# Rows transposed unscaled, mask tiles among the projections, and w1's product from high and low parts

## The reference

```
weights = x @ router_w + router_b            # per token
topi    = top 512 tokens of each batch; 511 of them, sorted, are selected
x_sel   = x[sel];  w_sel = weights[sel];  m_sel = mask[sel, sel]
hn      = x_sel * rsqrt(mean(x_sel^2) + 1e-6) * ln1
q, k, v = rope(hn @ wq), rope(hn @ wk), hn @ wv       # 16 heads of 16
o       = softmax(q k^T / 4 + m_sel) v @ wo
x1      = x_sel + o
x2      = x1 + gelu(rmsnorm(x1, ln2) @ w1) @ w2       # w1: 256 x 1024
out     = LayerNorm(x + scatter(x2 * w_sel) + x * (1 - sel_mask))
```

## Time and profile before

| | |
|---|---|
| median of 3 runs | 522.49 us (522.30 to 522.64) |
| profiled execution: its time, its span | 524.21 us, 522.5 us |
| PE busy | 437.1 us (84%) |
| PEld busy | 322.6 us (62%) |
| DVE busy | 389.2 us (74%) |
| ACT busy | 288.0 us (55%) |
| POOL busy | 173.0 us (33%) |
| chain that ended last, by engine | PE 39%, issue 14%, DVE 12%, POOL 9%, ACT 5% |
| chain, by line (largest) | L905 9%, L974 6%, L920 5%, L892 5%, L981 4% |

### The profile page before, as it was taken

How to read it: one execution, slowest core, us unless ns; L and a number is a source line. 1 busy time by engine, 2 the same in 40 slices (tenths; PEclk the granted TensorE clock), 3 DMA queues, 4 the chain that set the end, 5 groups by cost and what they waited for, 6 DMA issues and landing times.

```text
span 522.5 us, 9872 instructions
## 1 busy us (share of the span) xinstructions
PE 437.1 (84%) x3362; PEld 322.6 (62%) x3362; DVE 389.2 (74%) x1212; ACT 288.0 (55%) x611; POOL 173.0 (33%) x210
## 2 busy tenths in 40 slices
PE   3698999897999532698888999998998999997970
PEld 3487888786888422565675666664685666663560
DVE  2787888799888789667379999958368999956050
ACT  2335646444654460015688999944577999942200
POOL 9156677676767630552223000001000000003231
PEclk9999999998999855599998999998999999997995
DMA  7713432342231210249640000000000000000100
GB/s 224 235 42 82 123 120 82 118 124 81 82 121 42 80 41 1 85 150 316 204 134 2 1 3 3 3 1 0 1 1 2 2 2 3 1 2 10 32 30 11
DMA packets 29913, 33.90 MB, mean 65 GB/s; under 512 B 6404, under 2 KB 25512, under 8 KB 29864
## 3 DMA queue, kind: packets, MB, share of 16 engines
q1 hardware_dynamic: 23088, 24.78, 14.6%
q0 software_dynamic: 3520, 8.40, 5.4%
q10 hardware_dynamic: 3256, 0.10, 0.4%
HBM read 19.63 MB, written 13.63 MB: 64 GB/s over the span
## 4 chain that ended last, share of the span: by engine, by line
PE 39%; issue 14%; DVE 12%; POOL 9%; ACT 5%; another core or an unknown queue 1%; POOLq 1%; DVEq 0%; ACTq 0%
PE ps L905 9%; PE ps L974 6%; PE ps L920 5%; PE ps L892 5%; PE ps L981 4%; POOL arena L493 3%; PE ps L842 3%; PE ps L861 3%; POOL r L502 1%; PE ps L756 1%; POOL h_parts L552 1%; POOL rq L507 1%; PE ps L846 1%; DVE arena L1337 1%
## 5 line engine op out<-in xcount | busy, mean ns | idle before, releaser
L1184 ACT ACTIVATE arena<-arena,nmax 128x511 f32<-128x511 f32 x128 | 91.6, 720 | 5.6 <-DVE nmax L1609 5.3
L1609 DVE CUSTOM_DVE_ANT_0 arena<-ps,nmask 128x511 f32<-128x511 f32 x128 | 84.8, 684 | 0.2 <-DVE nmask L1557 0.2
L905 PE MATMUL ps<-ident,arena 128*128 128x128 f32 x512 | 80.0, 279 | 2.8 <-ACT big L397 1.1
L905 PEld LDWEIGHTS ps<-ident,arena 128*128 128x128 f32 x512 | 60.0, 142 | 24.5 <-ACT arena L1184 13.4
L683 PE MATMUL ps<-wgd_hi,x_hi 128*128 128x512 f32 x128 | 51.9, 405 | 0.0
L892 PE MATMUL ps<-arena 96*128 96x512 bf16 x128 | 49.1, 389 | 1.9 <-DVE nmask L1557 1.1
L684 PE MATMUL ps<-wgd_lo,x_hi 128*128 128x512 f32 x128 | 50.6, 395 | 0.0
L685 PE MATMUL ps<-wgd_hi,x_lo 128*128 128x512 f32 x128 | 50.5, 395 | 0.0
L397 DVE COPY big<-ps 128x512 f32<-128x512 f32 x64 | 44.1, 689 | 5.2 <-PE ps L905 3.9
L493 POOL TENSOR_TENSOR arena<-arena 128x512 f32<-128x512 f32 x32 | 41.2, 1290 | 12.7 <-DVE arena L1288 11.1
L397 ACT COPY big<-ps 128x512 f32<-128x512 f32 x64 | 37.0, 577 | 8.3 <-PE ps L920 6.6
(11 more groups left out here) (236 smaller groups left out, 994.5 us busy)
## 6 DMA issues: line engine op xcount, KB each, us to landing
arena<-in_L_attn_x SPq DMA_DIRECT2D x16, 512.0 KB, 4.6
out<-ob_sb SPq DMA_DIRECT2D x16, 512.0 KB, 3.2
w_sb<-in_L_ffn_w SPq DMA_DIRECT2D x2, 1024.0 KB, 11.5
mt_scratch<-nmask SPq DMA_DIRECT2D x8, 256.0 KB, 3.0
mt_scratch<-big SPq DMA_DIRECT2D x8, 256.0 KB, 3.8
big<-in_L_attn_Wg SPq DMA_DIRECT2D x1, 256.0 KB, 4.3
big<-in_L_attn_WD SPq DMA_DIRECT2D x1, 256.0 KB, 4.9
wqk<-in_L_ffn_wq SPq DMA_DIRECT2D x1, 256.0 KB, 8.8
```

What stands on the lines that cost most here:

```text
L905: mm = pe.transpose(ps[:, 2 + u % 2, k * P:(k + 1) * P], pr[u % 4][:, k * P:(k + 1) * P], ident[:, :])
L1184: act.activation(pr[u % 4][:, 0:K - 1], sm[u % 4][:, 0:K - 1], ACT.Exp, bias=nmax[:, c, h:h + 1], scale=-1.0, accum_out=rsum[:, c, h:h + 1 ...
L1609: dve.tensor_tensor_reduce(sm[u % 4][:, 0:K - 1], ps[:, S_BANKS[u % AHEAD], 0:K - 1], nmask[b][:, c, 0:K - 1], 1.0, 3.4e38, ALU.add, ALU.m ...
```

## The change

It does four things. The gathered rows are transposed as they come (`x_sel` in place of `hn`), and the factor per row (`wf_sel[..., 2]`, one per partition) is multiplied in by the copies of q, k (ACT) and v (DVE) out of PSUM; `first_normalised` goes, and `copy_qk` gets a wait for `angle_ready[b]`. `one_hots` builds `at_lo` and the two values of the row numbers first, `at_hi` next and the other 13 values last, and POOL starts the gathers on the first index tile. The mask's tiles of batch 0 are put among batch 1's first projections, in three banks; chunks 2 and 3 of batch 1 are transposed ahead of batch 1's tiles. The product with w1 is made of three float32r terms from `w1_hi`, `w1_lo` and `hnT_hi`, `hnT_lo`; the first two blocks have their low term last. The scratch of the selection moves from `qk[0]` to `v_sb[1]` and `x_sel[1]`.

```diff
+        w1_lo, = under(("w1_lo", [P, KD, F], F32R))
         w1_sb = sb("w1_sb", [P, KD, F])
+        w1_hi = sb("w1_hi", [P, KD, F], F32R)
...
+        hnT_hi, = under(("hnT_hi", [P, KD, K], F32R))
         hnT = sb("hnT", [P, KD, K])
+        hnT_lo, = under(("hnT_lo", [P, KD, K], F32R))
         qk = [sb(f"qk{b}", [P, C, 2 * D]) for b in range(B)]
         hi_rep = qk[1][:, :, :].rearrange("p c d -> p (c d)").bitcast(BF16)[:, 0:P * NT].rearrange("p (h n) -> p h n", h=P)
-        early_qk = qk[0][:, :, :].rearrange("p c d -> p (c d)")
+        v_sb = [sb(f"v_sb{b}", [P, C, D]) for b in range(B)]
 
         def scratch(at, n, dt=F32):
-            return early_qk[:, at:at + n].bitcast(dt)
+            tile, at = (v_sb[1], at) if at < 992 else (x_sel[1], at - 992)
+            return tile[:, :, :].rearrange("p c d -> p (c d)")[:, at:at + n].bitcast(dt)
...
-        R_BANK, REST_BANK = (2, 0), (4, 1)
+        R_BANK, REST_BANK = (2, 0), (1, 1)
+        X_BANK = ((2, 3), (3, 3))
...
-            pool.wait_ge(rows_ready[0], 3)
...
             def kept(b):
-                pool.wait_ge(hn_ready[b], C)
+                pool.wait_ge(angle_ready[b], 1)
                 for c in range(C):
+                    pool.wait_ge(x_sel_in[b][c], 16)
                     pool.tensor_scalar(keep[b][:, c, :], x_sel[b][:, c, :], wf_sel[:, b, c, 1:2], keep_m[:, b, c:c + 1],
...
-            gather_x(0)
-            gather_mask_rows(0)
-            pool.wait_ge(rows_ready[1], 3)
-            gather_x(1)
-            gather_mask_rows(1)
-            gather_mask_columns(0)
-            gather_mask_columns(1)
+            for b in range(B):
+                pool.wait_ge(rows_ready[b], 1)
+                gather_x(b)
+                pool.wait_ge(rows_ready[b], 2)
+                gather_mask_rows(b)
+            for b in range(B):
+                pool.wait_ge(rows_ready[b], 3)
+                gather_mask_columns(b)
...
-                pe.wait_ge(lo_ready[b], 1)
+                pe.wait_ge(lo_ready[b], 1 if hi == 2 else 2)
...
+                if b > 0:
+                    pe.wait_ge(angle_ready[b - 1], 1)
...
-            def turn_mask_rows(b):
+            def turn_mask_rows(b, tiles):
                 pe.wait_ge(m_rows_in[b], 16 * C)
-                for n in range(MS // P):
+                for n in tiles:
                     tile = n + b * (MS // P)
-                    if n == 0:
-                        pe.wait_ge(hnT1_ready[b], C)
-                    if b == 0 and n == 2:
+                    if tile == 0:
+                        pe.wait_ge(hnT1_ready[0], C)
                         pe.wait_ge(angle_ready[1], 1)
-                    if tile >= 4:
-                        pe.wait_ge(mT_ready[(tile - 4) // (MS // P)], (tile - 4) % (MS // P) + 1)
+                    elif tile >= 3:
+                        pe.wait_ge(mT_ready[(tile - 3) // (MS // P)], (tile - 3) % (MS // P) + 1)
                     for c in range(C):
-                        mm = pe.transpose(ps[:, (n + 2) % 4, c * P:(c + 1) * P], m_rows[b][:, c, n * P:(n + 1) * P], ident[:, :])
+                        mm = pe.transpose(ps[:, tile % 3, c * P:(c + 1) * P], m_rows[b][:, c, n * P:(n + 1) * P], ident[:, :])
                     mm.then_inc(mT_done[b], 1)
...
             def turn_first_hn(b, c):
-                pe.wait_ge(hn_ready[b], c + 1)
-                if c + b * C >= 2:
-                    pe.wait_ge(hnT1_ready[(c + b * C - 2) // C], (c + b * C - 2) % C + 1)
-                if b > 0:
-                    pe.wait_ge(mT_ready[b - 1], MS // P)
+                pe.wait_ge(x_sel_in[b][c], 16)
+                if b == 0 and c >= 2:
+                    pe.wait_ge(hnT1_ready[0], c - 1)
+                elif b == 1:
+                    pe.wait_ge(hnT1_ready[1], c)
                 for k in range(KD):
-                    mm = pe.transpose(ps[:, 2 + c % 2, k * P:(k + 1) * P], hn[:, c, k * P:(k + 1) * P], ident[:, :])
+                    mm = pe.transpose(ps[:, X_BANK[b][c % 2], k * P:(k + 1) * P], x_sel[b][:, c, k * P:(k + 1) * P], ident[:, :])
                 mm.then_inc(hnT1_done[b], 1)
...
             def hidden(b):
-                for f in range(FB):
-
-                    if f >= 2:
-                        pe.wait_ge(gelu_ready, b * FB + f - 1)
+                def with_high(f):
                     for k in range(KD):
                         pe.wait_ge(hnT_ready, b * KD + k + 1)
-                        mm = pe.matmul(ps[:, 4 + f % 2, :], w1_sb[:, k, f * P:(f + 1) * P], hnT[:, k, :],
-                                       start=(k == 0), stop=(k == KD - 1))
+                        for w in (w1_hi, w1_lo):
+                            pe.matmul(ps[:, 4 + f % 2, :], w[:, k, f * P:(f + 1) * P], hnT_hi[:, k, :],
+                                      start=(k == 0 and w is w1_hi), stop=False)
+
+                def with_rest(f):
+                    for k in range(KD):
+                        pe.wait_ge(hnT_lo_ready, b * KD + k + 1)
+                        mm = pe.matmul(ps[:, 4 + f % 2, :], w1_hi[:, k, f * P:(f + 1) * P], hnT_lo[:, k, :],
+                                       start=False, stop=(k == KD - 1))
                     mm.then_inc(h1_done, 1)
+
+                pe.wait_ge(w1_lo_ready, KD)
+                for f in range(2):
+                    with_high(f)
+                for f in range(2):
+                    with_rest(f)
+                for f in range(2, FB):
+                    pe.wait_ge(gelu_ready, b * FB + f - 1)
+                    with_high(f)
+                    with_rest(f)
...
-            turn_mask_rows(0)
-            for c in range(2):
+            turn_mask_rows(0, range(3))
+            turn_first_hn(1, 0)
+            project(1, range(1))
+            turn_mask_rows(0, range(3, 5))
+            turn_first_hn(1, 1)
+            project(1, range(1, 2))
+            turn_mask_rows(0, range(5, 8))
+            for c in range(2, C):
                 turn_first_hn(1, c)
-            for c in range(2):
-                project(1, range(c, c + 1))
-                turn_first_hn(1, 2 + c)
-            turn_mask_rows(1)
+            turn_mask_rows(1, range(8))
+            pe.wait_ge(hnT1_ready[1], C)
             pe.wait_ge(mT_ready[1], MS // P)
...
+            for k in range(KD):
+                act.wait_ge(w_ready, k + 1)
+                act.copy(w1_hi[:, k, :], w1_sb[:, k, :]).then_inc(w_ready, 1)
...
             def copy_hnT(b):
                 for k in range(KD):
                     act.wait_ge(hnT_done, b * KD + k + 1)
-                    act.copy(hnT[:, k, :], ps[:, 2 + k, :]).then_inc(hnT_ready, 1)
+                    act.copy(hnT_hi[:, k, :], ps[:, 2 + k, :]).then_inc(hnT_ready, 1)
 
             def copy_qk(b, c):
                 act.wait_ge(qk_done[b], c + 1)
-                act.copy(qk[b][:, c, :], ps[:, 4 + c % 2, :]).then_inc(qk_ready[b], 1)
+                act.wait_ge(angle_ready[b], 1)
+                act.mul(qk[b][:, c, :], ps[:, 4 + c % 2, :], wf_sel[:, b, c, 2:3]).then_inc(qk_ready[b], 1)
...
-                    act.mul(m_turned[b][n], ps[:, (n + 2) % 4, :], -1.0).then_inc(mT_ready[b], 1)
+                    act.mul(m_turned[b][n], ps[:, (n + b * (MS // P)) % 3, :], -1.0).then_inc(mT_ready[b], 1)
...
-            sines(0)
             for c in range(2):
                 copy_first_hnT(0, c)
+            sines(0)
             copy_qk(0, 0)
             for c in range(2, C):
                 copy_first_hnT(0, c)
                 copy_qk(0, c - 1)
             copy_qk(0, C - 1)
+            copy_mask_rows(0, range(3))
+            copy_first_hnT(1, 0)
+            copy_qk(1, 0)
+            copy_mask_rows(0, range(3, 5))
+            copy_first_hnT(1, 1)
+            more_parts(0, 0)
+            copy_qk(1, 1)
+            copy_mask_rows(0, range(5, 8))
+            for c in range(2, C):
+                copy_first_hnT(1, c)
+            copy_mask_rows(1, range(5))
+            more_parts(0, 1)
+            copy_mask_rows(1, range(5, 8))
             sines(1)
-            copy_mask_rows(0)
-            for c in range(2):
-                copy_first_hnT(1, c)
-            more_parts(0, 0)
-            for c in range(2):
-                copy_first_hnT(1, 2 + c)
-                copy_qk(1, c)
-            more_parts(0, 1)
-            copy_mask_rows(1)
...
             def one_hots(b):
-                dve.tensor_tensor(at_hi[:, b], slot_b[:, b, 0:1, :].broadcast_to((P, P, NT)), hi_rep[:, :, :],
-                                  ALU.is_equal).then_inc(at_ready[b], 1)
                 step.link(dve.tensor_tensor(
                     at_lo[:, b], slot_b[:, b, 1:2, :].broadcast_to((P, C, NT)),
                     lo_row[:, :].rearrange("p (c o) -> p c o", o=1).broadcast_to((P, C, NT)), ALU.is_equal))
+
+                def place(v0, v1):
+                    dve.tensor_tensor(
```

(47 more changed lines are left out.)

8 lines of the change are left out of this document (4 added, 4 removed).

## The result

The change made the kernel faster, by less than was forecast. Nine runs of the new kernel have a median of 519.19 us (516.68 to 521.22), nine of the old one beside them 522.49: a ratio of 0.9939 [0.9918, 0.9961], 3.3 us less where 8.2 were predicted. 519.19 lies 0.6 above the range. The profiled execution took 517.93 us (span 516.2, mean granted clock 0.931).

What follows compares the result with a forecast made beforehand. PE alone was taken to bound the product with w1, a chain walking between engines the stretch from the picks; 3.8 (Parts 1 and 2) + 2.3 + 2.3 = 8.4, taken as 8.2, gave 514.3 us, range 511.0 to 518.6.

Steps and rivals of the forecast that it cites:

- Part 3: Product with w1: three float32r products take 0.70 us where a float32 one took 0.86; 2.3 us less per batch, 4.6 in all.
- in either kernel: Product with w1: both stretches begin at the low clock, which costs some 2 us in the old and the new kernel.
- one that was too small (0.35): Product with w1: new wait of 0.35 us per batch, as gelu of block 0 needs its low term first.
- The cover of `rest_of_w1`: DVE before 349.20: two subtractions, 2.4 us together, fit in 3.07 us of idle, with 0.6 of room.
- Rival (b): The front's gain comes, the product's does not, as gelu or the low clock eats it: 518.7 us, chance 0.05.
- (d): Product with w1: weight loads and float32r products don't overlap, so the change is slower: 529.6 us, chance 0.03.
- Part 1: Picks of batch 0 to its transposes: first projection 4.4 us earlier, PE at the mask's tiles 3.7 earlier (235.5).
- Part 2: Mask's tiles: new order 18.7 us, 1.3 more than before, from a start 5.1 earlier; `turn_split(0, 0)` at 255.0, 3.8 earlier.
- an ACT that idled 7.50 us until 240.68 with a releaser that the profile doesn't know: Mask's tiles: the old first copy waited for this ACT idle, so the start gains more than PE does.
- From `turn_split(0, 0)` to attention nothing changes but the start.: Behind the mask's tiles: the 3.8 us gained up to `turn_split(0, 0)` carry on to attention unchanged.
- a clock that stays low past 224: Sign in the profile after, early projections: a clock still low past 224 us would show the forecast wrong.
- Rival (a): Front's gain swallowed by a wait in the interleaved mask part, later clock rise or ACT idle: 517.9 us, chance 0.14.

Runs made afterwards that it cites:

- product_only: The kernel before with only the product with w1 made of float32r terms, its front the old one: 518.16 us, ratio 0.9909.
- spread_gap_turns: The changed kernel with batch 1's picks spread among batch 0's projections and 16 unneeded transposes before the first `turn_split`: 514.60 us, ratio 0.985 to the kernel before.
- r_before: The kernel before, run again without edit: 522.70 us, ratio 1.0007.
- front_only: The changed kernel with the old float32 product with w1: 523.58 us, ratio 1.0013 to the kernel before.
- r_after: The changed kernel, run again without edit: 519.45 us, ratio 0.9935 to the kernel before.
- old_order: The changed kernel with the mask's tiles and batch 1's projections in the old order on PE and ACT: 516.71 us, ratio 0.9874 to the kernel before.
- front_old_order: The changed kernel with only the early transposes and `one_hots`: old float32 product, mask's tiles in the old order: 520.86 us, ratio 0.9963 to the kernel before.
- spread_old_order: The changed kernel with batch 1's picks spread and the mask's tiles in the old order: 514.22 us, ratio 0.9857 to the kernel before.

## Why the prediction was right and wrong

**Part 3 was right in its sum, partly by luck.** 4.6 us were forecast and `product_only` has 4.8, give or take 1. Products lie 0.23 us apart as in the earlier trace rows, and 48 take 13.2 us as forecast, where the stretch begins at the low clock. But the low clock doesn't cost 2 us "in either kernel". In the first batch of `spread_gap_turns` the clock is 1.00 throughout and the 48 products still take 367.50 - 355.00 = 12.5 us. The chain, `spread_gap_turns`:

```profile
356.36 1.21 DVE hnT_lo L1577 x2
...
357.61 0.51 PE ps L1013
...
358.15 0.61 ACT big L1273
```

At that clock PE is ready for `hnT_lo` before DVE, which does `rope(1, 0)` first, has it; the first 12 products take 358.80 - 355.00 = 3.80 us for 12 x 0.2325 = 2.79, so 1.0 us of waits in place of 0.35. At the low clock the eight products ahead take 3.36 us, `hnT_lo` is there in time, and 0.22 us of idle for gelu is left. So the low clock costs 0.7 us in the new product: a term that was too large (2) and one that was too small (0.35) made up for each other. By the profiles the two products take 14.97 + 15.68 us in `r_before` and 13.21 + 13.16 in the kernel after, 4.3 less, and 12.49 + 12.59 in `product_only`, 5.6 less.

The cover of `rest_of_w1` held; DVE's timeline, kernel after:

```profile
345.01 2.35 DVE L1543 TENSOR_TENSOR w_lo<-w_sb,w_hi 128x1024 fp32r<-128x1024 f32 x2
348.17 0.69 DVE L1673 TENSOR_TENSOR onT<-arena,ps 128x512 f32<-128x512 f32 x1 [0.81 <-ACT arena L1223]
```

2.35 us for the 2.4 assumed, and of 3.07 us of idle 0.81 are left. Rival (b) falls, and so does (d): the Trainium skill ("TensorE: Matmul & The Clock Gate", what overlaps and what doesn't) lets a load overlap a running product only when the row groups differ, and a load and a product of 128 rows each, every 0.23 us, don't agree with that.

**Part 1 was right in its times.** Against `r_before` the first projection comes 4.5 us earlier (223.22 to 218.71; forecast 4.4), in the low clock as assumed (3.41 us), `pick_rows(1)` 4.0 earlier (forecast 4.4), and PE reaches the mask's tiles at 237.2, where `r_before` has 235.23 + 3.31 + 1.72 + 0.86 = 241.1 by its own rows, 3.9 earlier (3.7). The copies with a factor per row take 0.69 us for 0.59 before. That is the 93 ns of the Trainium skill ("ScalarE: Activation LUTs", "What ACT_TABLE_LOAD costs") within 0.01. They cost next to nothing, as taken: one of them lies on the chain, ahead of the last `turn_split`, where it holds it up for 0.58 us in place of 0.48.

**Part 2 was right in its sum and wrong in what it was compared with.** From PE's arrival to `turn_split(0, 0)` 19.5 us were laid out (235.5 to 255.0); the profile has 237.2 to 256.56, 19.4. But the earlier trace rows hold a stall of ACT that the old kernel doesn't have as a rule: it took 19.65 from 239.16 there, and in `r_before` 259.34 - 241.1 = 18.2. A gain from "an ACT that idled 7.50 us until 240.68 with a releaser that the profile doesn't know" was counted that isn't there. `turn_split(0, 0)` is 2.8 us earlier, not 3.8. The new order is 1.2 longer than the old by this, as reckoned; with 1.6 for the clock behind it that makes 2.8, which the three pairs of kernels in the two orders (2.6, 3.2, 2.3) bear out within their error.

**The step that failed** is the sentence behind Part 2: "From `turn_split(0, 0)` to attention nothing changes but the start." It does, for the interleaving ends in 2.48 us without work for PE, and the clock falls behind them; the forecast had no term for that. Of 2.8 us at 256.6, 1.1 are left at the last `turn_split` (270.26 against 271.34 in `r_before`). Of these, 0.6 more go with the fall at the start of the first attention, and 0.5 are left at the product with w1 (356.85 against 357.34). The first fall is shown to come of the gap: it is in all five profiles in which the gap stands, and in none of the six with a changed front in which the gap is filled or the order is the old one. That the one in the attention follows from it is not shown: it is in all five as well and in none of the three of a filled gap, but it is in three others too.

**A second loss** was not in the text at all, or only as "a clock that stays low past 224" in another meaning: the clock falls again behind each pick of batch 1 in a part of the executions, some 3.4 us for the two; none of the three profiles with the old front has it. The sums go like this: 3.8 forecast, less 1.0 of a stall that wasn't, less 1.6 behind the gap (1.1 in the `turn_split`, 0.5 in the projection), less 0.6 at the start of the attention, less 3.4 in about half of the executions (8 of 16 of the change, 5 of 12 of `front_only`), 1.7 in the mean: 1.1 us lost, and `front_only`'s 1.0013 is 0.7 lost, give or take 1.1. That all runs at 0.924 or 0.925 are those with falls behind the picks is read from one profile of such a run of the interleaved order and from the distance of the groups (2.4 us in `r_after`, 2.9 in `front_only`, by their means); for the other runs it is an inference, for the mean clock tells how many falls there were and not where. That spreading the picks cures it is well supported: one of the 18 runs with spread picks is at 0.927 or under, against 23 of the 63 of the changed front without the spreading, and none of three profiles has the fall against three of eight.

Rival (a), "a wait in the interleaved mask part, a later clock rise", is nearest in place and time: 517.9 with a chance of 0.14. It took the front's whole gain away and had no term for a loss beyond it. With the clock kept, `spread_gap_turns` takes 514.60 us where 514.3 were predicted, but that agreement is partly luck: by the profiles its front is 2.3 us ahead of `r_before` at the product with w1 (355.00 against 357.34), not 3.8, and from there to the end it gains 5.6 more, not 4.6. The range ended at 518.6, 0.7 above that rival; a clock of 0.50 stands within the very stretch that was rebuilt, and what a rebuilt order does to it had no width in the range.

**Open**: why the old kernel, whose picks are the same 32 and 32 products, shows no fall behind them in its profiles and has no run at 0.927 or under, of the 64 of the three sets. In its two profiles the pick starts 1.2 and 1.4 us behind the rise of the clock (worked out from windows of 1 us); in the three that fall it is 0.9 to 1.3, and in the others of the new front 0.3 to 0.7, so that alone doesn't tell them apart. And what decides between the executions of one kernel: behind the picks, at the start of the attention, behind an idle of 1.4 us in the old front, and in the opening microseconds.

## What to carry to other kernels

When an order is rebuilt, list PE's idle times of the new order behind which it has dense work, and cost the first microseconds behind each at 1.2 GHz, if only as a width of the range; filling such a gap with needless work was worth 1.8 us (products) and 2.9 us (transposes) by the ratios, where the whole front was meant to bring 3.8. Don't count a stall of one profiled execution as a gain unless a second profile has it. When the kernel's runs fall into groups, compare the mean granted clock of the groups before looking for a cause in the work. And a total that comes out right needs its terms measured too: that of the product did so with two of them off.

## What the runs showed of the hardware

An idle of 2.06 to 2.49 us of TensorE, after work at 2.4 GHz, was followed by a granted clock of 0.52 to 0.68 in a window of 3 us behind it in each of the five profiles that have it; idles of 0.74 and 0.85 us at the same place, 1.29 in the kernel before, and 1.87 in the old order (ahead of the mask's last tiles, in `old_order`, `front_old_order` and `spread_old_order`) were not. Nor is the idle's length all: one of 1.42 us in `product_only` was followed by 0.50 for 3 us, one of 1.44 at the same place of the same work in `r_before` was not, and behind idles of 1.14, 0.27 and 0.46 us at the start of the first attention the clock fell in 8 profiles of 14. Sixteen 128x128 transposes in that idle kept the clock as ten products of 512 columns did. The clock can fall with no idle time in the profile too: 32 products of 8 columns, or of 52, were followed by 0.50 in a window of 2 us in three profiled executions, and not in the five others of a changed front; eight at a time between large products were followed by it in none of three. At the start products came 0.43 us apart, twice the usual, in 10 profiled executions of 14, of either kernel, while the granted clock in the record stands at 1.00 there.
